# A gather round on one core: POOL's wait ahead of a group is for the rows two groups ahead instead of one

## The reference

```python
xw = x @ W
ew = edge_attr @ edge_w            # 16 -> 128 for each edge
msg = xw[src] * ew
out = segment_sum(msg, dst, num_segments=x.shape[0]) + b
x = layernorm(x + out)
```

## Time and profile before

| What | Value |
|---|---|
| median of 3 runs (lowest to highest) | 5223.94 us (5223.72 to 5233.0) |
| profiled execution, its own time | 5221.52 us |
| its span in the profile | 5219.6 us |
| POOL busy | 2503.3 us (48%) |
| PE busy | 3551.5 us (68%) |
| DVE busy | 2338.9 us (45%) |
| mean granted clock | 0.81 |

### The profile page before, as it was taken

How to read it: one execution, slowest core, us unless ns; L and a number is a source line. 1 busy time by engine, 2 the same in 40 slices (tenths; PEclk the granted TensorE clock), 3 DMA queues, 4 the chain that set the end, 5 groups by cost and what they waited for, 6 DMA issues and landing times. The chain is left out here.

```text
span 5219.6 us, 66479 instructions
## 1 busy us (share of the span) xinstructions
PE 3551.5 (68%) x22480; PEld 2311.7 (44%) x22480; DVE 2338.9 (45%) x5012; ACT 1325.8 (25%) x3052; POOL 2503.3 (48%) x2412
## 2 busy tenths in 40 slices
PE   3777777777676766665333333336777999999997
PEld 3444444444344544444222222226774555555554
DVE  6444444444355656554455454446773131121303
ACT  1122222222222222222334334434663010000101
POOL 3666666666477777775777777771110000000001
PEclk7888888898788888888555555557998999999998
DMA  3223333333233333332666666666776767867674
GB/s 91 83 85 104 108 96 95 109 105 99 91 91 100 93 98 102 98 103 85 170 193 186 185 189 190 186 190 217 248 245 230 305 226 302 306 232 304 221 304 156
DMA packets 509160, 863.94 MB, mean 166 GB/s; under 512 B 111675, under 2 KB 284775, under 8 KB 508868
## 3 DMA queue, kind: packets, MB, share of 16 engines
q1 hardware_dynamic: 345136, 545.24, 29.7%
q0 software_dynamic: 90496, 189.62, 14.4%
q10 hardware_dynamic: 73236, 125.49, 6.4%
HBM read 632.93 MB, written 227.18 MB: 165 GB/s over the span
## 5 line engine op out<-in xcount | busy, mean ns | idle before, releaser
L731 POOL DMA_INDIRECT big<-xw_rows,srci x784 | 804.4, 1026 | 538.0 <-DMA big<-xw_rows,srci 235.8
L1596 PE MATMUL psS<-big,xsb 128*128 128x448 f16 x2744 | 971.7, 354 | 16.3 <-issue 8.5
L1596 PE MATMUL psA<-big,xsb 128*128 128x448 f16 x2744 | 971.6, 354 | 0.0
L763 POOL DMA_INDIRECT big<-axt_rows,srci x784 | 801.5, 1022 | 264.4 <-issue 233.6
L731 POOL DMA_INDIRECT big<-ht_rows,reli x784 | 786.2, 1003 | 277.7 <-issue 229.8
L1340 PE MATMUL psS<-big 128*128 128x128 f32 x3136 | 529.7, 340 | 318.6 <-DMA big<-ht_rows,reli 314.9
L1340 PEld LDWEIGHTS psS<-big 128*128 128x128 f32 x3136 | 502.7, 252 | 403.2 <-DMA big<-ht_rows,reli 352.2
L1476 PE MATMUL ps<-identh,xsb 128*128 128x128 bf16 x784 | 101.5, 311 | 598.6 <-DVE xsb L2082 598.6
L1401 PE MATMUL ps<-xsb,attrT 128*128 128x512 f32 x392 | 287.1, 873 | 288.7 <-DVE big L1909 288.3
L796 POOL DMA_DIRECT2D x_rows<-y x12 | 11.3, 946 | 961.4 <-DVE y L2339 943.7
L2296 DVE SCALAR_TENSOR_TENSOR acc<-psS,invs,acc 128x448 f32 x56 | 38.3, 684 | 914.5 <-PE psA L1596 914.5
(11 more groups left out here) (273 smaller groups left out, 5008.7 us busy)
## 6 DMA issues: line engine op xcount, KB each, us to landing
big<-A_rows SPq DMA_DIRECT2D x112, 2744.0 KB, 13.8
A_rows<-xsb ACTq DMA_DIRECT2D x196, 416.0 KB, 2.6
xg_rows<-big SPq DMA_DIRECT2D x98, 512.0 KB, 3.9
big<-xg_rows SPq DMA_DIRECT2D x98, 512.0 KB, 3.7
marks_rows<-big SPq DMA_DIRECT2D x98, 354.0 KB
big<-marks_rows SPq DMA_DIRECT2D x98, 354.0 KB, 4.5
big<-srcq_list SPq DMA_DIRECT2D x98, 256.0 KB
ht_rows<-big ACTq DMA_DIRECT2D x28, 512.0 KB, 2.8
```

Of the source, the lines that this page charges most:

```text
L731: pool.indirect_dma_start(ring[g % len(ring)][:, j * D:(j + 1) * D], None, table[:, :], bass.IndirectOffsetOnAxis(ap=lists[:, g * TPG + j: ...
L763: pool.indirect_dma_start(wide[g % NS][:, j, :], None, axt_rows[:, :], bass.IndirectOffsetOnAxis(ap=srci[:, g * TPG + j:g * TPG + j + 1], ...
L1596: m = pe.matmul(sums, xs[:, t, k, :], Aring[:, r, :, t, :], start=(t == 0), stop=(t == NB - 1))
```

## The change

POOL's second wait ahead of group g now begins at g = 2, and is for the landing of group g - 2. The wait for the message of g - 2 ahead of it, the number of DMAs, their order and their slots stay.

```diff
             for g in range(NG):
                 if g >= NEAR:
                     pool.wait_ge(s_msg[(g - NEAR) % 2], (g - NEAR) // 2 + 2)
-                if g:
-                    rows_landed(g - 1)
+                if g >= 2:
+                    rows_landed(g - 2)
                 gather_group(g, xw_rows, srci, slots)
```

## The result

The changed kernel takes 4981.6 us (median of 4 runs, 4978.76 to 4986.14), against 5223.83 us for the kernel before. The ratio is 0.9536, with a 95% interval of 0.9525 to 0.9547. The profiled execution took 4982.36 us, 239.2 us less than the one before.

What follows compares the result with a forecast made beforehand. The prediction took POOL's issue with its landing latency in series to bound the first round; 5223.9 us less 208.1 us of landing waits gave 5015.8 us, ratio 0.960, in a range of 4975 to 5060 us.

Steps and rivals of the forecast that it cites:

- The bound and the mechanism: First round: POOL's eight DMAs, one landing and a restart add up in each group; the second round is bound by issue alone.
- The main term: First round from group 2: 236.6 us of landing waits become ordinary gaps of 0.30 us, freeing 208.1 us.
- The new wait at zero: POOL's wait for the landing of g - 2 costs nothing, since the message wait before it already covers it.
- the unchanged start and second round: The first two groups gain nothing, and the second round keeps its pace of 10.46 us a group.
- the step on the first groups: Group 2 waits 10.12 us for the message of group 0, and longer by as much as group 1 is issued earlier.
- The duration of the DMAs: First round: DMAs meeting DVE's line 1817 cost some 0.45 us a group; bounds 165 to 267 us saved.
- the second round's pace: Check on the first round: 1003 us over 767 intervals, 1013 us with ten gaps added, the same as by subtraction.
- The low end of the forecast's own range: The forecast, chance 0.82, had its own range of 4958 to 5059 us; the low bound supposes no stretched DMA.
- The ten long gaps: Ten gaps of 1.3 us between POOL's DMAs in mid-group of the first round, counted at 1.0 us each.
- the rival of PE setting the pace: First round: each group needs PE's 10.78 us and a 0.3 us start, so the kernel takes 5069 us; chance 0.07.
- The rival of fast operations: DVE's lines 1851 and 1854 hold POOL, 2.15 us more a group, nearly the gain, so 5220 us; chance 0.02.

Runs made afterwards that it cites:

- the eight comparisons: Line 1817 made as eight one-input comparisons in the first round, against the kernel waiting for g - 1 behind the group's first DMA: 5125.5 us, ratio 0.9817.

## Why the prediction came out as it did

- **The bound and the mechanism** were right. The landing latency stood in series with POOL's issue and nothing covered it. Half of the waits gave half of the gain, and a wait behind two DMAs costs nothing.
- **The main term** was right to 0.1 us: 208.1 forecast, 208.0 measured. It had to be, once every wait went and left the ordinary gap; that they all went is what the prediction got right. The new wait at zero was right (4981.7 us without it), and so were the unchanged start and second round; group 2 waited 2.2 us longer, as the step on the first groups had it.
- **The duration of the DMAs** is the term that was mis-sized. The prediction kept the stretch at 0.45 us a group, with bounds from none to double. It measured 0.24 us where 0.47 us was, 21.8 us in the sum. I had the reason, that another DMA meets line 1817, and the trace of the kernel before had the rows to place it. One of them, the message of the earlier trace rows's group:

```profile
299.06 1.22 DVE L1909 TENSOR_TENSOR big<-big,ps 128x1024 f32<-128x1024 f32 x1 [8.28 <-DMA big<-xw_rows,srci]
```

With the earlier trace rows they give 1.52 us from the last DMA's end to the message and 1.33 us on to line 1817 (its start at 300.39 against the message's at 299.06), 2.85 us after that end; the next group's third DMA starts 0.30 + 2 x 1.24 = 2.78 us after it, just ahead. The changed kernel has this: the third DMA at 400.97, line 1817 at 401.19, and only the fourth DMA, at 402.22, starts inside it, 0.20 us before its end of 402.42, and takes 1.03 us. The agreement with the second round's pace, which I took as a check, held by chance: that round has its own phase and one more two-input operation. (The low end of the forecast's own range, 5223.9 - 267, is 4957 us and not 4958.)
- **The ten long gaps** were counted as staying, 10 us, since the first round has them and the second hasn't. They went with the waits. The runs tie them to waits that aren't met (ten with 95, five with 47, none with none, and none with as many waits that are all met) and to fixed places of the program, every ninth group; what they are stays open.
- **PE.** I had 0.9 us of wait a group or a little more; it is 1.5 us, as the clock rose. Nothing spoke for the rival of PE setting the pace: DVE's message waits for rows alone in the window, and never for PE's edge factors.
- **The rival of fast operations** named lines that can hold a DMA, for 2.1 us beyond its 0.94 us, but in the changed kernel they don't: no DMA takes over 1.9 us there from group 3 on. The Trainium skill (SBUF — State Buffer, A bandwidth-pool intuition that's wrong (but worth ruling out)) gives about 115 ns from the end of a blocking VectorE operation to the end of the blocked DMA; the 0.11 and 0.12 us behind the chains agree, though each chain is ten operations and not one, and the 0.82 us behind a two-input operation don't. The Trainium skill (SBUF — State Buffer, Who interferes with whom) infers that a two-input `tensor_tensor` doesn't hold up the writing of descriptors, but it also has such an operation contend with a GpSimd instruction that reads SBUF, which the prediction left out. Here it does stretch an indirect DMA: one that starts inside it ends 0.82 us after it.

## What to carry to other kernels

A wait for a landing that stands at the end of a train of DMAs costs its whole latency each time, here 2.2 us of it; behind as much of the engine's own issue as the latency is long it costs nothing, so ask how far back a wait must look and not whether it is needed. When the pace of an engine changes, its phase against the others changes too: a cost that comes from two instructions meeting must be placed anew on the timeline, not carried over. An edit that shortens or splits the instruction that holds another can let a longer hold through.

## What the runs showed of the hardware

- An indirect DMA on POOL (128 rows of 512 bytes) takes 0.94 us, and there are 0.30 us to the next. One that starts inside a DVE operation with two inputs in SBUF ends 0.82 us after that operation: at 302.43, 465.36 and 513.79 us in three kernels. In the kernel before, 98 DMAs of the first round take over 1.0 us from group 2 on; 90 start inside such an operation, and 89 of these end 0.81 to 0.83 us after it (the other is the one at 132.03). The other eight start inside line 1851 and take at most 1.08 us. Inside line 1909, which has one input in SBUF and one in PSUM, 96 DMAs start, and none takes over 0.96 us.
- One that starts just ahead of a gapless chain of fast one-input DVE operations can be held until 0.11 or 0.12 us after the whole chain, 3.00 and 3.15 us instead of 0.94 us, and in one kernel 14 DMAs that started inside the chain's first 0.40 us ended 0.81 to 0.83 us after it. With the eight comparisons ahead of the chain 47 of 78 DMAs were held so; with line 1817 ahead of it none of 81. Which condition decides stays open.
- Seen from PE, the matmuls of line 1401 went from a median of 990 ns to 593 ns in these windows (344 and 348 records) as PE's wait ahead of them fell from 2.97 to 1.5 us a group.
